# Rearranging the fill of the latent attention, and scaling the routed attention's output per head behind its out-projection

## The reference, cut to what matters

```
def _L0_ffn_ref(...):            # routed: 4 of 16 heads per batch, 64 wide
    score = softmax(einsum('bhqd,bhkd->bhqk', Qs, Ks) * scale, axis=-1)
    O = einsum('bhqk,bhkd->bhqd', score, Vs)
    O = O.transpose(0, 2, 1, 3).reshape(b, s, N_ACTIVE * D_ATTN)
    return O @ Wo + bo
...
def _L2_xattn_ref(...):          # 2 heads; keys: 512 latents and 77 context tokens
    q, k, v = split_heads(ln @ Wq.T), k and v of concat(ln @ Wlkv.T, xn @ Wkv.T)
    attn = softmax(rmsnorm(q) * SCALE @ rmsnorm(k).T, masked)
    return (attn @ v) @ Wo.T + bo
```

## Time and profile before

| | |
|---|---|
| median of 3 runs | 563.67 us (563.59 to 565.5) |
| the profiled execution's own time | 562.91 us |
| its span, first to last instruction | 560.9 us |
| TensorE / DVE / ACT / POOL busy | 86% / 69% / 48% / 28% of the span |
| mean granted TensorE clock | 0.927 |
| routed attention, first score to the last tile's moments | 182.9 to 244.4 us |
| folding of chunks 3 to 7 | 293.0 to 304.7 us |
| latent projections | 305.2 to 321.1 us |
| latent attention's first steps | 322.1 to 342.2 us |

### The profile page before, as it was taken

How to read it: one execution, slowest core, us unless ns; L and a number is a source line. 1 busy time by engine, 2 the same in 40 slices (tenths; PEclk the granted TensorE clock), 3 DMA queues, 4 the chain that set the end, 5 groups by cost and what they waited for, 6 DMA issues and landing times. The chain is left out here.

```text
span 560.9 us, 9297 instructions
## 1 busy us (share of the span) xinstructions
PE 480.3 (86%) x3121; PEld 336.1 (60%) x3121; DVE 384.7 (69%) x1365; ACT 269.0 (48%) x819; POOL 155.1 (28%) x185
## 2 busy tenths in 40 slices
PE   2940699999979999988886958989999999889987
PEld 2410599897634666775555436756666666658945
DVE  3799979844683767844779476863543646789876
ACT  2798488512325666613455334642222221679643
POOL 4999983031135400002104440111000000020042
PEclk9755579999999999997898889999999999989999
DMA  7104000002191000000012300000000000000001
GB/s 264 58 1 150 1 4 1 2 0 71 81 384 46 2 1 2 1 2 1 0 35 58 90 1 1 2 0 2 2 0 1 0 1 1 1 1 1 2 0 39
DMA packets 8453, 18.37 MB, mean 33 GB/s; under 512 B 1171, under 2 KB 6611, under 8 KB 7894
## 3 DMA queue, kind: packets, MB, share of 16 engines
q1 hardware_dynamic: 8406, 17.78, 9.0%
HBM read 15.99 MB, written 1.79 MB: 32 GB/s over the span
## 5 line engine op out<-in xcount | busy, mean ns | idle before, releaser
L212 POOL TENSOR_SCALAR rtmp<-mv 128x4 f32<-128x4 f32 x18 | 4.4, 246 | 240.2 <-DVE mv L191 209.6
L1875 PEld LDWEIGHTS bank<-arenaA,arenaB 128*128 128x128 f32 x320 | 38.7, 192 | 8.4 <-issue 7.2
L1859 PE MATMUL bank<-xnT,arenaA 128*128 128x512 f32 x80 | 41.1, 595 | 0.7 <-ACT xnT L270 0.7
L1886 ACT ACTIVATE xt<-bank 128x512 f32<-128x512 f32 x26 | 15.6, 599 | 54.3 <-PE bank L1859 53.1
L1937 DVE TENSOR_TENSOR arenaB<-xt,bank 128x512 f32<-128x512 f32 x26 | 17.8, 686 | 34.5 <-PE bank L1860 31.8
L1860 PE MATMUL bank<-xnT,arenaA 128*128 128x512 f32 x80 | 40.9, 592 | 0.0
L1875 PE MATMUL bank<-arenaA,arenaB 128*128 128x128 f32 x320 | 38.8, 275 | 0.0
L263 PE MATMUL bank<-in_ctx 128*128 128x512 f32 (+1 forms) x94 | 32.3, 485 | 0.0
L1100 DVE TENSOR_REDUCE nmax<-bank 128x1 f32<-128x512 f32 x32 | 20.5, 684 | 13.2 <-PE bank L1043 13.2
L428 DVE MATCH_REPLACE8 arenaB<-arenaB 128x77 f32<-128x77 f32 x128 | 26.8, 222 | 0.0
L1860 PEld LDWEIGHTS bank<-xnT,arenaA 128*128 128x128 f32 x80 | 15.2, 190 | 19.1 <-issue 19.1
(11 more groups left out here) (486 smaller groups left out, 1306.9 us busy)
## 6 DMA issues: line engine op xcount, KB each, us to landing
arenaA<-in_moe_dram SPq DMA_DIRECT2D x1, 3840.0 KB, 11.6
in_dft<-in_dft_dram SPq DMA_DIRECT2D x1, 2048.0 KB, 7.5
in_dft<-in_head_dram SPq DMA_DIRECT2D x1, 2048.0 KB, 7.6
arenaA<-in_l_dram SPq DMA_DIRECT2D x1, 2048.0 KB, 16.1
vw_scratch<-in_dft SPq DMA_DIRECT2D x32, 38.5 KB
arenaB<-vw_scratch SPq DMA_DIRECT2D x2, 576.0 KB, 4.9
in_rows<-in_rows_dram SPq DMA_DIRECT2D x1, 842.5 KB, 7.3
in_ctx<-in_ctx_dram SPq DMA_DIRECT2D x1, 653.0 KB, 6.3
```

The source lines that it names most:

```text
L1859: nc.tensor.matmul(bank[n % 2][:], w[:, c * P:(c + 1) * P], xnT[:, b * S:(b + 1) * S], start=True, stop=True).then_inc(up_mm, 1)
L1875: ins = nc.tensor.matmul(bank[4 + m % 2][:, q4 * P:(q4 + 1) * P], hid2[:, m % 2, c, q4 * P:(q4 + 1) * P], w[:, 2 * HE + c * P:2 * HE + (c ...
L1886: nc.scalar.activation(sil2[n % 3], bank[n % 2][:], ACT.Silu).then_inc(silu_ready, 1)
```

## The change

In the routed attention the broadcast of 1/sum is gone (the matmul L1058, ACT's copy L1145) and so is DVE's multiplication L1114. ACT copies unscaled O of unit n-2 to SBUF instead, behind the exponentials of unit n. PV always goes to bank 6. The out-projection becomes four matmuls of 64 rows, one a head, each to a place of its own (banks 3 and 7). DVE adds each head's share with `scalar_tensor_tensor`, scaled by that head's 1/sum: four instructions a tile, each waiting for the one before it, and they stand behind the copy of the transposed probabilities. The scores use three banks by turns, so that each waits for the exponential three scores before.

In the folding a filler of 256 columns stands before the second matmuls of chunks 3 to 7, and one of 512 columns before the latent tiles are turned. In the latent attention the first score of step 1 no longer waits; a filler of 512 columns and then the second score come behind the wait for the first exponential. The turning of batch 1's q and k moves from the end of step 1 behind the scores of step 2, and a filler takes its place. POOL adds the bias row after step 0. The counts of `rinv_ready` stay; `rb_mm` and `rb_copy` are counted from 0 in the latent attention.

```diff
--- before.py
+++ after.py
         NU = NT * 2
+        score0 = lambda n, i: bank[(2 * n + i) % 3]
+        Y0 = lambda i, c: bank[3 + 4 * (1 - i)][:, c * P:(c + 1) * P]
...
                     b = t // TB
-                    if n >= 2:
-                        pe.wait_ge(sc_exp, 2 * (n - 1))
                     for i in range(2):
+                        if 2 * n + i >= 3:
+                            pe.wait_ge(sc_exp, 2 * n + i - 2)
                         r = slice(DF * i, DF * (i + 1))
-                        nc.tensor.matmul(bank[2 * (n % 2) + i][:], qT[r, b, pair, (t % TB) * P:(t % TB + 1) * P],
+                        nc.tensor.matmul(score0(n, i)[:], qT[r, b, pair, (t % TB) * P:(t % TB + 1) * P],
                                          kT[r, b, pair, :], start=True, stop=True).then_inc(sc_mm, 1)
                 if n == 1:
...
                 m = n - 2
                 if 0 <= m < NU:
                     t, pair = m // 2, m % 2
-                    own, other = bank[6 + m % 2], bank[6 + (m + 1) % 2]
-                    pe.wait_ge(rinv_ready, m + 1)
-                    if m:
-                        pe.wait_ge(o_norm, m)
-                    else:
-                        pe.wait_ge(v_ready, 4)
-                    for i in range(2):
-                        h = 2 * pair + i
-                        ins = nc.tensor.matmul(other[DF * i:DF * (i + 1), AT_R], rinv0[:, t, h:h + 1].broadcast_to([P, DF]), ident,
-                                               start=True, stop=True)
-                    ins.then_inc(rb_mm, 1)
                     pe.wait_ge(pT_dve, m + 1)
                     pe.wait_ge(pT_act, m + 1)
                     if m:
-                        pe.wait_ge(rb_copy, m)
-                    if pair and t:
-                        pe.wait_ge(x_added, t)
+                        pe.wait_ge(oT0_copy, m)
+                    else:
+                        pe.wait_ge(v_ready, 4)
                     for k in range(TB):
                         for i in range(2):
                             h = 2 * pair + i
-                            ins = nc.tensor.matmul(own[DF * i:DF * (i + 1), AT_O], vv0[:, t // TB * TB + k, h * DF:(h + 1) * DF],
+                            ins = nc.tensor.matmul(bank[6][DF * i:DF * (i + 1), 0:P], vv0[:, t // TB * TB + k, h * DF:(h + 1) * DF],
                                                    pT0[:, m % 2, i, k * P:(k + 1) * P], start=(k == 0), stop=(k == TB - 1))
                     ins.then_inc(pv_mm, 1)
                 if 2 <= m <= NU and m % 2 == 0:
                     t = m // 2 - 1
-                    pe.wait_ge(o_norm, m)
-                    pe.wait_ge(rb_copy, min(m + 1, NU))
+                    pe.wait_ge(oT0_copy, m)
+                    if t:
+                        pe.wait_ge(x_added, t)
                     for c in range(2):
-                        ins = nc.tensor.matmul(bank[7][:, AT_W], oT0[:, (2 * t + c) % 4, :], wo0[:, c * P:(c + 1) * P],
-                                               start=(c == 0), stop=(c == 1))
+                        for i in range(2):
+                            r = slice(DF * i, DF * (i + 1))
+                            ins = nc.tensor.matmul(Y0(i, c), oT0[r, (2 * t + c) % 4, :], wo0[r, c * P:(c + 1) * P], start=True, stop=True)
                     ins.then_inc(wo_mm, 1)
...
                         dve.wait_ge(sc_mm, 2 * n + i + 1)
-                        Vv.tensor_reduce(nmax0[:, t, h:h + 1], bank[2 * (n % 2) + i][:], AX.X, ALU.max, negate=True).then_inc(sc_max, 1)
+                        Vv.tensor_reduce(nmax0[:, t, h:h + 1], score0(n, i)[:], AX.X, ALU.max, negate=True).then_inc(sc_max, 1)
...
                     vec_v0(dve, 1)
-                m = n - 2
-                if 0 <= m < NU:
-                    dve.wait_ge(rb_copy, m + 1)
-                    dve.wait_ge(pv_mm, m + 1)
-                    if m >= 4:
-                        dve.wait_ge(wo_mm, m // 2 - 1)
-                    Vv.tensor_tensor(oT0[:, m % 4, :], bank[6 + m % 2][:, AT_O], rb0[:, m % 2, :], ALU.mult).then_inc(o_norm, 1)
-                if 2 <= m <= NU and m % 2 == 0:
-                    t = m // 2 - 1
-                    if t == 0:
-                        dve.wait_ge(row_added, 2)
-                    dve.wait_ge(wo_mm, t + 1)
-                    Vv.tensor_tensor(X[:, t, :], bank[7][:, AT_W], tmp[:, t, :], ALU.add).then_inc(x_added, 1)
                 m = n - 1
                 if 0 <= m < NU:
                     dve.wait_ge(sc_turned, 2 * m + 1)
                     if m >= 2:
                         dve.wait_ge(pv_mm, m - 1)
                     Vv.tensor_copy(pT0[:, m % 2, 0, :], bank[4][:]).then_inc(pT_dve, 1)
+                m = n - 2
+                if 2 <= m <= NU and m % 2 == 0:
+                    t = m // 2 - 1
+                    if t == 0:
+                        dve.wait_ge(row_added, 2)
+                    dve.wait_ge(rinv_ready, 2 * t + 2)
+                    dve.wait_ge(wo_mm, t + 1)
+                    for h in range(4):
+                        ins = Vv.scalar_tensor_tensor(X[:, t, :], Y0(h % 2, h // 2), rinv0[:, t, h:h + 1],
+                                                      X[:, t, :] if h else tmp[:, t, :], ALU.mult, ALU.add)
+                        if h < 3:
+                            st.link(ins)
+                    ins.then_inc(x_added, 1)
...
             for n in range(NU + 2):
-                m = n - 2
-                if 0 <= m < NU:
-                    act.wait_ge(rb_mm, m + 1)
-                    if m >= 2:
-                        act.wait_ge(o_norm, m - 1)
-                    nc.scalar.copy(rb0[:, m % 2, :], bank[6 + (m + 1) % 2][:, AT_R]).then_inc(rb_copy, 1)
...
                         act.wait_ge(sc_max, 2 * n + i + 1)
-                        nc.scalar.activation(pb0[:, n % 2, i, :], bank[2 * (n % 2) + i][:], ACT.Exp, bias=nmax0[:, t, h:h + 1],
+                        nc.scalar.activation(pb0[:, n % 2, i, :], score0(n, i)[:], ACT.Exp, bias=nmax0[:, t, h:h + 1],
                                              accum_out=rsum0[:, t, h:h + 1]).then_inc(sc_exp, 1)
+                m = n - 2
+                if 0 <= m < NU:
+                    act.wait_ge(pv_mm, m + 1)
+                    if m >= 4:
+                        act.wait_ge(wo_mm, m // 2 - 1)
+                    nc.scalar.copy(oT0[:, m % 4, :], bank[6][:, 0:P]).then_inc(oT0_copy, 1)
...
             pe.wait_ge(l1f_act, NT // 2 + 7)
-            pe_fold3(pe, *FOLD3[2])
+            pe_fold3(pe, *FOLD3[2], S // 2)
...
             at = NB * DC
-            pe_fold3(pe, *FOLD3[3])
+            pe_fold3(pe, *FOLD3[3], S // 2)
+            pe_spin(1, 1, S)
...
                     b = n // TB
-                    if n:
-                        pe.wait_ge(a2_exp, H2 * (n - 1) + 1)
                     for h in range(H2):
+                        if H2 * n + h >= 3:
+                            pe.wait_ge(a2_exp, H2 * n + h - 2)
                         r = slice(D2 * h, D2 * (h + 1))
+                        if n == 1 and h == 1:
+                            pe_spin(5, 1, S)
                         nc.tensor.matmul(score2(n, h)[:], qT2[r, n * P:(n + 1) * P], kT2[r, b * S:(b + 1) * S], start=True, stop=True).then_inc(a2_mm, 1)
                 if n == NT + 1:
                     pe_turn(pe, ln_done, NT * 8, xn, [0])
                 if n == 2:
+                    pe_turn_qk2(pe, 1, (6, 7))
...
                     ins.then_inc(a2_turned, 1)
                 if n == 1:
                     pe.wait_ge(c2_added, 1)
-                    pe_turn_qk2(pe, 1, (6, 7))
+                    pe_spin(6, 1, S)
...
                 nc.gpsimd.tensor_tensor(pc2[:, n % 2], ctx2(n), bc(nm2[:, n, :], P, H2, NC), ALU.add).then_inc(a2_shift, 1)
-                if n == 1:
+                if n == 0:
                     pool_bias(pool, 7, V["bo2"], row_added)
...
-        def pe_fold3(pe, first, last):
+        def pe_fold3(pe, first, last, width=0):
...
                 c = n - 1
                 if c >= first:
                     cc = slice(c * P, (c + 1) * P)
+                    if width:
+                        pe_spin(1, 1, width)
                     pe.wait_ge(kv3_copy, 2 * c + 2)
```

11 lines of the change are left out of this document (5 added, 6 removed).

## The result

The changed kernel takes **569.39 us** (median of 5 runs, 567.99 to 572.31), the kernel before 563.85 (5 runs): a ratio of **1.0106, 95% interval 1.0076 to 1.0135**. It is slower by 1%, 5.5 us, where 564.9 and no change were forecast. The profiled execution is the longest of the five (572.31, its span 570.4), and the one before is 0.9 under its median, so the 9.5 us between the two spans hold about 4 that the medians don't.

A forecast was written before the change was run, and what follows sets the result against it. TensorE was taken as the bound almost everywhere, with DVE, POOL and ACT holding it up around the latent stages. 562.91 + 6.1 - 2.25 - 2.65 = 564.1, plus 0.76 for the median: 564.9 us, range 558.5 to 569.0.

The forecast's parts named there:

- Part 1: Routed attention: saved broadcasts are lost because the loop through DVE and ACT lengthens; +6.1 us in all.
- the start: Routed attention's first steps: second score of step 1 waits for the first exponential, delaying what follows; +1.5 us.
- The tile: Two steps of routed attention: 7.14 becomes 7.5 through the DVE and ACT loop; 0.36 over six tiles, +2.2 us.
- Normalising four tiles in the chain: Routed attention, step 12: this DVE work, formerly in idle time, now stands in the loop behind the additions; +1.1 us.
- The tail: End of routed attention: four additions for one behind the last projection, a copy for a multiplication; +1.2 us.
- Rival 1: Routed attention: additions cost only DVE's idle time and TensorE stays the bound; 557.2 us in all, chance 0.15.
- its version by the rule of the Trainium skill: Routed attention: signals within the chain cost nothing, four additions take 1.12; 562.2 us, counted as no change, chance 0.12.
- Part 2: Folding and latent projections: fillers keep the clock at 1.00, so the first projections run faster; -2.25 us.
- so nothing is lost: Latent projections: POOL's norm for batch 1 ended at 312.94 against 313.0 wanted, so the gain of 2.25 stays whole.
- Part 3: Latent attention's first steps: moving POOL's bias row speeds DVE's scaling, 3.81 to some 1.7; -2.65 us.
- then the scores of step 2: Latent attention: these scores follow the scaling's end at 334.85 and last until 335.45, then q and k are turned.
- Rival 2: Folding and latent attention: clock falls at 305 despite fillers, folding ends 0.5 late, part 3 gains 1.5; 568.8 us, chance 0.2.

The follow-up runs named there:

- e1: Kernel before with only the routed attention changed, folding and latent attention as before: 571.14 us, ratio 1.0147.
- e2: Kernel before with only the folding's fillers and the latent attention's changes, routed attention as before: 563.54 us, ratio 0.9978.
- e10: Kernel before with only the folding's fillers and the one before the latent tiles: 563.45 us, ratio 0.9992.
- e4: Whole change with ACT's copy of O ahead of the exponentials in the odd steps: 568.89 us, ratio 1.0076.
- e7: Whole change with a tile's four scaled additions split, two where they were and two a step later: 564.94 us, ratio 1.0018.
- e8: e7 with the fourth score of all in bank 3: 562.56 us, ratio 0.9974.
- e11: Whole change with step 1's latent filler ahead of its wait and twice 512 columns: 565.45 us, ratio 1.0035.
- e3: Whole change with all four scaled additions one step later, between 1/sum and the copy of the probabilities: 568.34 us, ratio 1.0073.
- e15: e10 with two fillers of 512 columns at the start of the routed attention, a delay of 1.72: ratio 1.0072 to the kernel before.
- e16: e10 with three fillers of 512 columns at the start of the routed attention, a delay of 2.58: ratio 1.0066 to the kernel before.
- e5: e2 with a 512-column filler in each of two gaps before ACT's turned tiles, and five fillers for four behind the first projections: 562.53 us, ratio 0.9962.
- e6: e5 with step 1's latent filler ahead of its wait and twice 512 columns: 558.77 us, ratio 0.9902.
- e12: Routed attention of e8 together with the latent half of e6: 558.64 us, ratio 0.9903.

## Why the prediction was wrong

**Part 1 was right, and a little high.** +5.31 where +6.1 was forecast, by the terms: the start +1.85 (1.5), since the lone score costs 1.05 and not 0.86. The tile 7.35 (7.5), so 0.21 a tile for 0.36 and 0.9 less over six: the chain was the right one. Its largest miss is from the exponential to the copy of the probabilities, 1.34 + 0.15 for 1.49 + 0.28; the other terms are off by up to 0.09 either way and nearly cancel, which is luck. Normalising four tiles in the chain +1.03 (8.38 for 7.35 at that tile, PV at 231.51 and at 239.89; forecast 1.1). The tail +1.22 (1.2): 4.15 for 2.93 from the last PV to the last moments. The sure sign, PV waiting for ACT's copy in every second step, is in the rows. Rival 1, the short loop, is out. So is its version by the rule of the Trainium skill ("VectorE: DVE Perf Modes", section "The DRAIN you can't avoid") that a signal behind each instruction of a chain adds nothing: linked additions start 0.37 to 0.39 apart here (223.38 to 223.75, and three in 1.12), unlinked ones of the same form 0.26, so 1.49 for four (223.38 to 224.87) against 1.12. The linked four add to one tile and the unlinked ones to four; how much is the signal's and how much the wait's, no run here tells.

**The sum itself failed in that it holds changed stages alone.** 562.91 + 6.1 - 2.25 - 2.65 counts nothing for unchanged code. e1 shows +1.86 between the routed attention and the first projection, and +1.4 near 500 us went with the folding's fillers. In the trace of the change these are 1.80 and 1.41, so 3.2 of its 9.5; with the start's 1.56, likewise in unchanged code and within that row's scatter, half of all. The routed half, the latent half and these two make +7.9, against the 4.3 to 7.6 that the ratio's interval leaves for the typical run.

**Part 2: the term -2.25 was right (-2.33), "so nothing is lost" was not.** The forecast had the second projections at full clock as before, 3.39 to the squares. TensorE waited 0.54 for DVE, whose latents waited for POOL, and 0.87 for ACT, and the second projections took 4.54 for 2.85: 0.54 + 1.69 = 2.23 given back, and the first score of the latent attention came 17.34 behind the first projection, as before. The fillers' own length cost nothing: from the last moments to the first projection e2 and e10 took 62.5 for 62.79. Of eight traces with the folding's fillers and neither filled gaps nor a delay, the clock held through both pairs in five (e4, e7, e8, e10, e11) and failed in three (the change itself, e2, e3), and it failed in both with a delay (e15, e16, 4.54 again); with the gaps filled it held in all three (e5, e6, e12). At five of ten without, three of three with filled gaps don't yet show that the gaps are the cause. And even where it held, 1.4 were lost near 500 us, so that this part alone measured 0.9992.

**Part 3: the term -2.65 was -0.58.** The scaling (1.67) and the idle time before the filler (2.35, "some 2.3") came as forecast. The lower clock came only with the late score: the filler took 1.06 (1.7 forecast), the score 1.71 (1.7). So the scaling was done 9.62 behind the first score, earlier than the 10.29 forecast. The step that failed is "then the scores of step 2": I let them follow the scaling and forgot TensorE's own queue. Ahead of them stand step 1's transposes, the context's, and the second new filler, at the lower clock. They began 11.07 and ended 12.8 behind the first score, the forecast had 10.89 for their end. The chain had passed from DVE to TensorE, and there a filler in front of needed work costs its length, here 1.91. e6's 12.72 and e11's 12.73 for 17.05 show what the same stretch takes with step 1's filler ahead of the wait and at full clock throughout; the second filler stood where it was and took 1.02 in e6.

**The range and the rivals.** 569.39 is just outside 569.0. Rival 2 (568.8) is nearest by its number, and that is luck. Its part 2 isn't what happened: the clock did not fall at 305 but at 325, in the second batch, and the folding did not end late. Nor is its part 3 ("the filler and the late score at the lower clock eat more of the gain"): these two took 2.77 together where 3.4 were forecast, and the gain went in TensorE's queue behind them.

## What to carry to other kernels

An operation that is moved behind its matmul leaves TensorE but enters another engine's chain: write down the whole loop, PV to PV, before counting TensorE's saving, and where a block of small operations delays whatever stands behind it, split it over two steps. Put a filler ahead of the wait and not between the wait and the work that was waited for (here moved and doubled together, 4.3 us in one stretch), and ask for each filler what TensorE does next at the next gap, since a clock that is held up in one stage may fall in the next. Try the cheapest part by itself: one moved POOL instruction gave 0.6% (0.4% to 0.8%), more than the whole latent rearrangement that it came with.

## What was not expected of the hardware

- Taking the broadcasts away saved less than they had taken. Two of them were 0.54 a tile, yet with TensorE as the bound again the tile is 6.90 for 7.14. PV takes 1.02 to 1.03 from start to start for 0.97, the transposes behind it 1.02 to 1.03 for 0.96 to 0.98, and the four half-row products of the projection 0.65 for the 0.55 of the two full ones.
- A pure delay of 1.72 on the critical path cost 4.1 (1.0045 to 1.0101 as a ratio), and in its trace a part-busy stretch behind it ran 3.3 longer, with a granted clock of 0.50 from 286 to 290.
- Fillers between 293 and 305 us go with 1.6 more in one line of code near 500 us, in 13 traces of 13 and in none of the 5 without them; the same 13 have the longer wait just before it.
